# A four-layer attention and expert kernel: first loads reordered, row normalising and high parts of keys and values moved to ScalarE in layer 0, GpSimd's fence changed at layer 1

## The reference, cut to what matters

```
def _layernorm(x, axis=-1, eps=1e-05):
    m = jnp.mean(x, axis=axis, keepdims=True)
    v = jnp.var(x, axis=axis, keepdims=True)
    return (x - m) / jnp.sqrt(v + eps)
...
q = (text_hidden @ Wq).reshape(B, T_text, N_HEADS, HEAD_DIM)...
k = (vision_tokens @ Wk)...            # layer 0: 16 heads of 128, 8 key heads, each used by two
v = (vision_tokens @ Wv)...
scores = jnp.einsum('bhtd,bhsd->bhts', q, k) / scale
scores = jnp.where(mask, scores, -jnp.inf)
attn = jax.nn.softmax(scores, axis=-1)
out = jnp.einsum('bhts,bhsd->bhtd', attn, v)
return out @ Wo
```

## Time and profile before

| | us |
|---|---|
| median of 3 runs | 3810.18 |
| lowest and highest | 3809.44, 3819.05 |
| the profiled execution's own time | 3808.53 |
| span of the profile, first to last instruction | 3806.5 |
| PE busy | 3422.7 (90%) |
| DVE busy | 2425.4 (64%) |
| ACT busy | 1623.2 (43%) |
| POOL busy | 1295.1 (34%) |
| mean granted clock of PE | 0.958 |

### The profile page before, as it was taken

One profiled execution on the slowest core, in us unless ns is written; L12 is line 12 of the kernel. 1 busy time (PEld: TensorE's weight loads), 2 busy tenths in 40 slices (PEclk: granted clock), 3 DMA queues, 4 the chain that ended last, 5 costly groups with the idle time before them and its releaser, 6 DMA issues.

```text
span 3806.5 us, 62024 instructions
## 1 busy us (share of the span) xinstructions
PE 3422.7 (90%) x23446; PEld 2808.7 (74%) x23446; DVE 2425.4 (64%) x4746; ACT 1623.2 (43%) x3496; POOL 1295.1 (34%) x1212
## 2 busy tenths in 40 slices
PE   5999999968999589997999789998789999999977
PEld 5899998947777346655998645554589999999865
DVE  6778888863222368875444446665667777777766
ACT  3566665431111055552222245555245555555431
POOL 0003334202241477742222246665522222222212
PEclk9999999988999799998999889999989999999989
DMA  3236665114644110001000100000000000000001
GB/s 121 77 114 217 226 222 186 50 45 177 236 168 186 72 32 27 22 5 57 34 34 12 37 2 4 4 4 15 20 17 12 18 18 18 15 10 18 12 1 47
DMA packets 94468, 246.52 MB, mean 65 GB/s; under 512 B 14432, under 2 KB 18656, under 8 KB 89312
## 3 DMA queue, kind: packets, MB, share of 16 engines
q1 hardware_dynamic: 87936, 222.12, 16.9%
q0 software_dynamic: 6240, 20.45, 1.5%
HBM read 364.95 MB, written 70.52 MB: 114 GB/s over the span
## 4 chain that ended last, share of the span: by engine, by line
PE 39%; DVE 6%; issue 3%; ACT 2%; POOL 2%; DMA 0%; SPq 0%; POOLq 0%; DVEq 0%; ACTq 0%
PE banks L100 34%; PE banks L205 4%; ACT P L74 1%; POOL kst L83 0%; DVE xn L88 0%; DVE X L83 0%; DVE st L242 0%; DVE PL L83 0%; DVE X L91 0%; POOL rs L83 0%; DVE KL L91 0%; ACT nkT L77 0%; DVE P L87 0%; POOL CL L83 0%; DVE XL L83 0%
## 5 line engine op out<-in xcount | busy, mean ns | idle before, releaser
L83 DVE TENSOR_TENSOR X<-X,banks 128x512 f32<-128x512 f32 x352 | 240.3, 684 | 203.9 <-PE banks L100 203.4
L94 DVE TENSOR_REDUCE nmx<-banks 128x4 f32<-128x1024 f32 (+2 forms) x256 | 239.3, 956 | 158.7 <-PE banks L100 155.6
L100 PE MATMUL banks<-XH,wqh 128*128 128x256 f32 x1024 | 292.0, 285 | 0.0
L83 POOL TENSOR_TENSOR slo<-sraw,shi 128x512 fp32r<-128x512 f32 x96 | 126.7, 1320 | 472.6 <-ACT shi L77 465.2
L100 PE MATMUL banks<-XL,wqh 128*128 128x256 f32 x1024 | 286.3, 280 | 0.0
L100 PE MATMUL banks<-XH,wql 128*128 128x256 f32 x1024 | 286.1, 279 | 0.0
L100 PE MATMUL banks<-XH,tT 128*128 128x256 f32 x1024 | 245.8, 284 | 14.0 <-issue 6.6
L100 PE MATMUL banks<-XL,tT 128*128 128x256 f32 x1024 | 244.6, 283 | 0.0
L74 ACT ACTIVATE nPT<-banks 128x1024 f32<-128x1024 f32 x192 | 195.8, 1020 | 110.3 <-PE banks L100 108.5
L100 PE MATMUL banks<-woh,OH 128*128 128x512 f32 x512 | 219.1, 428 | 12.3 <-DVE OL L83 10.5
L74 ACT ACTIVATE P<-banks,nb,qst 128x256 f32<-128x256 f32 x256 | 141.2, 561 | 191.1 <-DVE nb L83 191.0
(11 more groups left out here) (425 smaller groups left out, 10581.2 us busy)
## 6 DMA issues: line engine op xcount, KB each, us to landing
WU<-expert_parts SPq DMA_DIRECT2D x39, 4096.0 KB
WD<-expert_parts SPq DMA_DIRECT2D x39, 2048.0 KB
sraw<-in_moe_w SPq DMA_DIRECT2D x96, 256.0 KB, 3.3
expert_parts<-shi SPq DMA_DIRECT2D x96, 256.0 KB
expert_parts<-slo SPq DMA_DIRECT2D x96, 256.0 KB
wqr<-in_L_xattn_Wq SPq DMA_DIRECT2D x16, 512.0 KB, 3.9
wor<-in_L_xattn_Wo SPq DMA_DIRECT2D x16, 512.0 KB, 5.6
sraw<-in_L_ffn_factors SPq DMA_DIRECT2D x32, 256.0 KB, 3.2
```

What stands on the lines that cost most here:

```text
L83: return self.e.tensor_tensor(out, a, b, op)
L94: return self.e.tensor_reduce(out, a, AX.X, op, **kw)
L100: return self.e.matmul(out, l, r, start=start, stop=stop, skip_group_check=skip)
```

## The change

Four parts. (1) SP asks for the first quarter of `X`, then the mask, the first key and value weights, the first 512 columns of `CTX`, the first query and output weights, the second quarter of `X`, and then the rest. (2) In layer 0's `ln` steps DVE makes statistics tile by tile, four before the first step and the others two tiles ahead; the inverse roots are per tile on POOL, which also makes `nm = -mean * rs`; ACT normalises, `xn = Identity(rs * X + nm)`. The mask's rows are made after `part` 0, and ACT starts with one `Exp` of a single column. (3) ACT copies `KH` and `VH`, ahead of `QH`; DVE's `KL` waits for `VH`. (4) At fence 2 POOL sets `om` and adds to the fence's semaphore in place of a drain; SP runs `sp_narrow_load(sp, 1)` behind the first two `gt` loads.

```diff
-EXPERTS = {..., "x1": 304}
+EXPERTS = {..., "x1": 304, "vd0": 16}
+WIDE_0 = {"vh": 64}
-LN_EACH = (2, 3, 4, 5, 6, 7)
-LN_AHEAD = (5, 6)
+LN_EACH = (0, 2, 3, 4, 5, 6, 7)
+LN_AHEAD = (0, 5, 6)
...
     def sp_start(self, sp):
...
-        for h in range(4):
+        def rows(h):
             sp.dma(self.X[:, 4 * h:4 * h + 4, :], x[:, 4 * h:4 * h + 4, :]).then_inc(S[f"x{h}"], 16)
-        sp.dma(self.CTX[:], self.ins["ctxT"]).then_inc(S["ctx"], 16)
+        rows(0)
+        sp.dma(w["mu8"][:], self.ins["mask_BxS2_bf1"].rearrange("(a b) s -> a (b s)", a=1).to_broadcast([128, T])
+               ).then_inc(S["load_a"], 16)
+        sp.dma(w["wk"][:, 0, :, :], self.ins[pre + "Wk"][0]).then_inc(S["wkv0"], 16)
+        sp.dma(w["wv"][:, 0, :, :], self.ins[pre + "Wv"][0]).then_inc(S["wkv0"], 16)
+        sp.dma(self.CTX[:, :, 0:512], self.ins["ctxT"][:, :, 0:512]).then_inc(S["ctx"], 16)
+        sp.dma(w["wqr"][:], self.ins[pre + "Wq"][0]).then_inc(S["wq"], 16)
+        sp.dma(w["wor"][:], self.ins[pre + "Wo"][0]).then_inc(S["wo"], 16)
+        rows(1)
+        sp.dma(self.CTX[:, :, 512:T], self.ins["ctxT"][:, :, 512:T]).then_inc(S["ctx2"], 16)
+        rows(2)
+        rows(3)
...
     def dve_start(self, dve):
...
-        for t in range(NT):
-            dve.wait_ge(S[f"x{t // 4}"], 16)
-            self.dve_stat(dve, 0, t)
+        for t in range(4):
+            self.dve_stat_in(dve, t)
...
     def dve_ln(self, dve, n, t, keep=None):
...
-        for k in ([0, 1] if t == 0 else [t + 1] if t + 1 < NT else []):
+        for k in ([0, 1] if t == 0 else [t + 1] if t + 1 < NT else []) if n else []:
             self.dve_ln_norm(dve, n, k, keep)
...
     def pool_ln(self, pool, n, t):
...
                 self.rsqrt(pool, self.rs[:, k:k + 1], self.sc1[:, k:k + 1]).then_inc(S["rs"], 1)
+                if n == 0:
+                    pool.wait_ge(S["rs"], ln_rs(0, k) - 1)
+                    pool.ts(self.nm[:, k:k + 1], self.mv[:, k, 0:1], self.rs[:, k:k + 1], -1.0, ALU.mult, ALU.mult
+                            ).then_inc(S["rs"], 1)
...
     def act_ln(self, act, n, t):
         S = self.S
+        for k in ([0, 1] if t == 0 else [t + 1] if t + 1 < NT else []) if n == 0 else []:
+            act.wait_ge(S["ln_turned"], k - 1)
+            act.wait_ge(S["rs"], ln_rs(0, k))
+            act.act(self.xn[:, k % 2, :], self.X[:, k, :], ACT.Identity, bias=self.nm[:, k:k + 1], scale=self.rs[:, k:k + 1]
+                    ).then_inc(S["xn"], 1)
...
     def act_wide(self, act, L):
...
+        if l0:
+            act.act(self.s48[:, 0:1], self.mhalf[:, 0:1], ACT.Exp)
...
+                if l0:
+                    k = banks[1]
+                    act.wait_ge(S["kvz"], u + 1)
+                    act.wait_ge(S["sc"], 2 * U)
+                    act.acopy(w["KH"][:, 0, :], k[:, 0:256])
+                    act.wait_ge(S["ov"], U - 1)
+                    act.acopy(w["VH"][:, u % 2, :, :], k[:, 256:512].rearrange("p (t n) -> p t n", t=2)).then_inc(S["vh"], 1)
...
     def dve_wide(self, dve, L):
...
             if step == "ln":
+                if l0 and 2 <= u < NT - 2:
+                    self.dve_stat_in(dve, u + 2)
                 self.dve_ln(dve, n, u)
             if step == "part" and u < 8:
                 self.dve_part(dve, L, u)
+                if l0 and u == 0:
+                    self.dve_mask(dve)
...
                 if l0:
-                    dve.wait_ge(S["kvz"], u + 1)
-                    dve.wait_ge(S["sc"], 2 * U)
-                    dve.copy(w["KH"][:, 0, :], k[:, 0:256]).then_inc(S["k0"], 1)
-                    dve.wait_ge(S["k0"], 4 * u + 1)
+                    dve.wait_ge(S["vh"], u + 1)
                     dve.tt(w["KL"][:, 0, :], k[:, 0:256], w["KH"][:, 0, :].bitcast(F32), ALU.subtract).then_inc(S["k0"], 1)
                     v = k[:, 256:512].rearrange("p (t n) -> p t n", t=2)
-                    dve.wait_ge(S["ov"], U - 1)
-                    dve.copy(w["VH"][:, j, :, :], v).then_inc(S["k0"], 1)
-                    dve.wait_ge(S["k0"], 4 * u + 3)
                     dve.tt(w["VL"][:, j, :, :], v, w["VH"][:, j, :, :].bitcast(F32), ALU.subtract).then_inc(S["k0"], 1)
...
     def sp_narrow(self, sp, L):
...
                 sp.dma(w["gt"][:, a % 2, :, :], back[a]).then_inc(S[f"x{2 + a % 2}"], 16)
+                if a == 1:
+                    self.sp_narrow_load(sp, 1)
...
+    def pool_leave_experts(self, pool):
+        pool.e.memset(self.W[1]["om"][:], 1.0).then_inc(self.S["fence"], 1)
+        pool.wait_ge(self.S["fence"], 10)
...
     def pool_narrow(self, pool, L):
...
-            pool.e.memset(w["om"][:], 1.0).then_inc(S["n_sel"], 1)
-            pool.wait_ge(S["n_sel"], c + 1)
...
     def pool_program(self, e):
...
-        self.fence(pool, 2)
+        self.pool_leave_experts(pool)
...
     def sp_program(self, e):
...
-        self.sp_narrow_load(sp, 1)
```

More of the change, by code:

```diff
@@ L44 @@
 CHOICE_ON = {"ctl": "gelu", "ctp": "hh", "cta": "down"}
+CTX_ON = {"ctx2": "vd0"}
 BLOCKS = {"gelu": NBLK, "hh": NBLK, "down": NBLK}
 CRANK, CBACK = (2, 5, 7), (4, 6, 8)
-EXPERTS = {"raw0": 1408, "raw1": 1408, "xs0": 1792, "xs1": 1536, "n_hik": 96, "n_lok": 96, "n_ek": 39, "n_eq": 39, "x1": 304}
+EXPERTS = {"raw0": 1408, "raw1": 1408, "xs0": 1792, "xs1": 1536, "n_hik": 96, "n_lok": 96, "n_ek": 39, "n_eq": 39, "x1": 304, "vd0": 16}
+WIDE_0 = {"vh": 64}
 NARROW_1 = {"n_qp": 16, "n_kp": 17, "n_vp": 16, "n_tq": 64, "n_tk": 64, "n_hiq": 32, "n_hik": 128, "n_loq": 32, "n_lok": 128,
             "n_eq": 103, "n_ek": 103, "n_st": 64, "n_sc": 64, "n_e": 64, "n_mx": 128, "n_pv": 32, "n_mt": 32, "n_mT": 32,
-            "xs0": 2048, "xs1": 1792, "n_o": 32, "n_r": 96, "n_y": 16, "n_vv": 16, "n_xa": 16, "n_xb": 16, "n_sel": 11}
+            "xs0": 2048, "xs1": 1792, "n_o": 32, "n_r": 96, "n_y": 16, "n_vv": 16, "n_xa": 16, "n_xb": 16, "n_sel": 10}
 class Eng:
@@ L124, with ln_var @@
 LN_SPLIT = {0: 0, 1: 1, 3: 2, 5: 3, 6: 4, 7: 5}
-LN_EACH = (2, 3, 4, 5, 6, 7)
-LN_AHEAD = (5, 6)
+LN_EACH = (0, 2, 3, 4, 5, 6, 7)
+LN_AHEAD = (0, 5, 6)
+def ln_var(n, t):
+    return sum(16 if k in LN_EACH else 1 for k in range(n)) + (t + 1 if n in LN_EACH else 1)
 def ln_rs(n, t):
-    return sum(16 if k in LN_EACH else 1 for k in range(n)) + (t + 1 if n in LN_EACH else 1)
+    return ln_var(n, t) + (16 if n else t + 1)
 def ln_xl(n, t):
@@ L152, in __init__ @@
         self.S = Sems(nc)
-        for name, first in CHOICE_ON.items():
+        for name, first in (CHOICE_ON | CTX_ON).items():
             self.S[name] = self.S[first]
@@ L171, in __init__ @@
         self.rs = self.sb("rs", [128, NT], F32)
+        self.nm = self.sb("nm", [128, NT], F32)
         self.st = self.sb("st", [128, NT, 6], F32)
@@ L229, in dve_start, with dve_stat_in @@
         dve.e.memset(self.ones[:], 1.0).then_inc(S["dve_one"], 1)
-        for t in range(NT):
-            dve.wait_ge(S[f"x{t // 4}"], 16)
-            self.dve_stat(dve, 0, t)
+        for t in range(4):
+            self.dve_stat_in(dve, t)
+    def dve_stat_in(self, dve, t):
+        dve.wait_ge(self.S[f"x{t // 4}"], 16)
+        self.dve_stat(dve, 0, t)
     def consts(self, e):
@@ L583, in sp_wide @@
         if l0:
-            sp.dma(w["mu8"][:], self.ins["mask_BxS2_bf1"].rearrange("(a b) s -> a (b s)", a=1).to_broadcast([128, T])
-                   ).then_inc(S["load_a"], 16)
             for i in range(2):
@@ L592, in sp_wide @@
                 self.sp_choice_early(sp)
-            if step == "fetch" and g < 8:
+            if step == "fetch" and g < 8 and not (l0 and g == 0):
                 self.sp_fetch(sp, L, g)
@@ L605, in sp_wide @@
             sp.wait_ge(S["ctx"], 16)
+            sp.wait_ge(S["ctx2"], 16)
     def pool_wide(self, pool, L):
@@ L647, in pe_wide @@
                     elif l0:
-                        pe.wait_ge(S["k0"], 4 * v + 4)
+                        pe.wait_ge(S["k0"], 2 * v + 2)
                     else:
@@ L658, in pe_wide @@
                 k = banks[1]
-                if u == 0:
-                    pe.wait_ge(S["ctx"], 16)
+                if u in (0, 2):
+                    pe.wait_ge(S["ctx2" if u else "ctx"], 16)
                 if l0:
@@ L663, in pe_wide @@
                         pe.wait_ge(S[f"wkv{j}"], 32 * (g // 2 + 1))
-                    pe.wait_ge(S["k0"], 4 * u)
+                    pe.wait_ge(S["k0"], 2 * u)
                     pe.mms(k[:, 0:256], [(w["wk"][:, j, c, :], self.CTX[:, c, tok]) for c in range(2)])
@@ L736, in pe_wide @@
                         pe.wait_ge(S["seed"], 2 * (u - 1) + qt + 1)
-                        pe.wait_ge(S["k0"], 4 * u + 4)
+                        pe.wait_ge(S["k0"], 2 * u + 2)
                     else:
@@ L857, in act_wide, with dve_mask @@
                 self.act_ln(act, 7, t)
+    def dve_mask(self, dve):
+        S, w = self.S, self.W[0]
+        dve.wait_ge(S["load_a"], ONE["mask"])
+        dve.red(w["anym"][:], w["mu8"][:].rearrange("p (b s) -> p b s", b=NB), ALU.max).then_inc(S["dve_one"], 1)
```

(9 more changed lines are left out.)

5 lines of the change are left out of this document (3 added, 2 removed).

## The result

| | before | after |
|---|---|---|
| median of 11 runs each | 3809.88 | 3793.87 |
| lowest and highest | 3805.59, 3819.05 | 3784.03, 3799.41 |
| span of the profile | 3806.5 | 3793.1 |
| PE busy | 3422.7 | 3446.5 |
| DVE busy | 2425.4 | 2369.5 |

The ratio is 0.9954, with a 95% interval of 0.9945 to 0.9964: faster by 16 us, where 38 were forecast, and above the top of the range (3788). The lines of the table say where to look: PE, which executes the same 23446 matmuls as before, was busy 23.8 us longer.

The account below looks back on a forecast made before the run. PE sets the pace in layer 0, with idle stretches at the start and before layer 1. Terms -16.5-4.5-2.5-15 = -38.5 from 3808.53 give 3770.0, 3771.7 against the median, stated as 3772; 3763 to 3788 holds 8 in 10.

Parts of the forecast that it names:

- start: Kernel start up to PE's first scores: scores at 28.2 instead of 45.13, -16.9 worked out, -16.5 taken.
- layer 0: PE's waits in layer 0 shrink: -4.5 for `QL` before scores and -2.5 for `xn` and `QL` before the turns.
- into layer 1: Experts to layer 1, no POOL drain: first addition at 1273.85 instead of 1289.30, -15.4, taken as -15.
- the second quarter of `X`: At the start: lands at 14.8, just before DVE comes at 15.1; rival that it or `wo` is late, 3780, 10 in 100.
- PE's waits for `QL` before scores: Layer 0, 11.7 us in 9 waits: each shrinks by at most 0.83 as DVE loses `KH` and `VH`, -4.5.
- Those for `xn`: Layer 0, PE's waits for `xn`: with those for `QL` before the turns, -2.5 of 13.1.
- an estimate of 4.3: Into layer 1, by the skill page: scatter counts at 1270, `gt` lands at 1273.7, term -15.3 without its 1.5 us margin.
- The rival in which ACT holds layer 0: Layer 0: ACT's two copies delay `KL`, `VL`, `QL` and `QH`, 77 us more, 3856; 2 in 100.
- the clock's dips: Layer 0's three low-clock dips, 5.1 us, were left in; rival that they go with shorter waits, 3767, 15 in 100.
- Everything after shifts as a whole.: Stages after layer 1's start: take the same time as before, so the earlier gains last to the end.
- the gain is given back: Later stages: waits set by transfers that do not move, or clock dips elsewhere, 3800 or more; 6 in 100.

Follow-up runs that it names:

- nm at the end: Changed kernel with the new 64-byte tile `nm` put at the end of the memory instead of between `rs` and `st`: 3781.03 us, ratio to before 0.9916.
- and drain in idle time: Kernel of nm at the end with one more POOL drain, behind its addition of the 28th output of layer 1's attention: 3770.16 us, ratio to before 0.9888.

## Why the prediction was right and wrong

How far ahead of the kernel before (negative) each profile is, split by stage (us, read on ACT at `QH` of the first and the 64th unit, on POOL at the last scatter, the first addition of `gt` and the last addition of layer 1, at DVE's first instruction behind fence 3, at POOL's last `tHL`, and at the first and the last `QH` of layer 3):

| stage | forecast | changed | nm at the end | and drain in idle time |
|---|---|---|---|---|
| start | -16.5 | -16.6 | -16.9 | -17.5 |
| layer 0 | -7.0 | -7.4 | -10.8 | -9.1 |
| experts | 0 | +4.6 | +3.6 | +1.9 |
| into layer 1 | -15.0 | -15.65 | -15.65 | -15.7 |
| layer 1 | 0 | +1.0 | +5.6 | +1.3 |
| fence 3 | 0 | +5.35 | +5.35 | 0.0 |
| ternary | 0 | +9.1 | +4.1 | +2.7 |
| layer 2 and mix | 0 | +1.6 | -2.7 | -2.7 |
| layer 3 | 0 | +4.1 | +0.7 | +0.6 |
| sum | -38.5 | -14.0 | -26.7 | -38.5 |

**Right.** The start and the way into layer 1, and layer 0 in its sum. The start: projection, scores and the order of DVE's work came within 0.6 us of the stated times, and the second quarter of `X` in time. Two prices missed in opposite directions there: `xn` on ACT took 0.82 us where 0.60 was put, `nm` 0.27 where 0.4 was. Layer 0: -7.0 was put, -7.4 came, but the split was wrong. PE's waits for `QL` before scores fell by 6.2 us where 4.5 were put. Those for `xn` fell by 1.1 and those for `QL` before the turns not at all, where 2.5 were put (the terms written down for them add up to 2.9). A dip of the clock that went (1.7 us) and the wider spacing, some 1.4 by the estimate above, about cancel. Into layer 1: -15.4 was worked out, -15.65 came, because `gt` landed before POOL's setup ended. SP could ask for it 3.24 us after POOL's last scatter (1249.52 and 1246.28), where 2.8 were put. By the Trainium skill (DMA: Bandwidth & Descriptors, Anatomy of one DMA — SWDGE (gpsimd) path), which puts most of 2.0 us between a transfer's last byte and its semaphore, the prediction had made an estimate of 4.3. The trace stands between the two and nearer to the sum: the windows show the scatter's bytes moving until 1248.5, and SP asked 1.0 us later. The rival in which ACT holds layer 0 was not seen, and the clock's dips went from three to two in layer 0.

**Wrong, first.** "Everything after shifts as a whole." The step put every later stage at 0, and it failed twice. What it missed most is the tile `nm`: I priced its 32 instructions at nothing and never asked where it stands. Placing it elsewhere gave 12.8 us. The Trainium skill (TensorE: Matmul & The Clock Gate, Step-by-step: what each phase is for) says that PE has two independent read ports, so that loading the next weights takes no read bandwidth from the running matmul. The traces here show that where the two operands stand matters all the same: 64 bytes more between the tiles that hold them moved the spacing of matmuls by 4% (114.1 and 118.9 ns in layer 3). Whether it is these two reads that meet, and in which part of the memory, was not measured.

**Wrong, second.** "POOL no longer drains": true, and the term is right, but the 7.6 us were not saved. They are owed once, and the next drain, at fence 3, paid them: 2.41 became 7.76. The rival "the gain is given back" had 6 in 100 and spoke of transfers; the place to look was the engine's own next drain.

**Luck.** With both mended, the last column sums to -38.5 like the forecast, and the median is 3770 against 3772. The single rows don't agree so well: layer 0 is 2.1 us better than put, the start 1.0, and the stages put at 0 sum to 3.8. That the totals meet is partly chance.

**What stays open.** From POOL's first instruction behind fence 1 to the last scatter the experts took 462.5 us before, 466.9 in the changed kernel and 459 to 471 in all the traces, of kernels whose instructions don't differ there. The low clock goes with it: 61 to 62 us of it with 459.2 and 460.1, 79 to 80 with 469.8 and 470.5. At half the rate, 18 us more of it are worth up to 9 us of PE's work, an estimate that comes near the 10 us between them. Layer 1 likewise takes either 464 to 467 us or 471, the longer with a lower clock at its beginning. The first 70.7 us of layer 1, in the kernel before and in the one with `nm` at the end:

```profile
1289.30:1360.00 70.70, 40.54 (x94) 18.12 (x95) 39.19 (x62) 13.34 (x26) 54.34 (x36) 0.77 0.12 40
```

```profile
1249.60:1320.30 70.70, 43.36 (x80) 17.48 (x80) 36.16 (x60) 10.94 (x21) 49.70 (x33) 0.71 0.22 81
```

The clock is 0.77 and 0.71. What makes an execution fall one way or the other wasn't found, so a difference of 4 us between two profiles means little in these two stages. The groups of layer 3 don't hang on them; medians of four or five executions may, by a few us.

## What to carry to other kernels

A new tile moves all that are allocated behind it. Where PE is the bound, compare the spacing of its matmuls between the two kernels in a stretch without waits before looking for lost waits, and put small additions at the end of the memory, or pad them to 256 bytes, which kept the good rate here. A drain that is left out may only be postponed: look at the next one, and put it where the engine idles anyway. Price an engine's gain to the end of the program, with one row at each fence, and not to the place where it appears.

## What the runs showed of the hardware

- Matmuls that take one operand from `XH` or `XL` and the other from `wqh` or `wql` came every 114.1 ns in layer 3 at the distances of the kernel before, and every 118.0 to 120.0 with the second operand 64, 128 or 192 bytes further on; at 256 and 512 bytes further they were fast again, and with both moved by 64 bytes too. With `tT` in the ternary stage it was 116.6 against 117.8 to 119.9, also where no other computing engine was at work. A weight group took 109.36 us at the good distances, between 109.34 and 109.38 behind the first one, in nine kernels.
- POOL's first drain behind its 78 gathers and scatters lasts 7.2 to 7.8 us, at once or 470 us later, and costs 5 to 6.5 us where something waits for it; the other drains of the same kernels last at most 1.9 us, and the one 968 us after its predecessor 0.65. At fence 3 a drain that is not the first takes 1.36 us (2.42 from POOL's last addition to DVE). Gathers and scatters were not told apart.
- Executions of unchanged code differ by up to 11 us in the experts' stage (459.2 to 470.5), and the time of low granted clock goes with it (61.6 and 79.6 us).
